# Attention stage of a decoder block: row maxima turned by a product in fp32r, and routing logits formed in four column groups

## What is computed

```
scores = einsum('bhqd,bhkd->bhqk', qh, kh) * scale
attn = softmax(scores, axis=-1)
out = einsum('bhqk,bhkd->bhqd', attn, vh)
x = x + concat @ Wo + bo
...
rh = gelu(layernorm(x) @ rW1 + rb1, approximate=False)   # 512 -> 1024
router_logits = rh @ rW2 + rb2                           # 1024 -> 4
```

## Time and profile before

| | us |
|---|---|
| median of 3 runs | 2783.26 (2781.48 to 2784.44) |
| profiled execution, its own time | 2773.2 |
| its span, first to last instruction | 2771.3 |
| mean granted TensorE clock | 0.935 of full |
| attention stage in the trace | about 1016 to 1851 |
| iterations 1 to 6, from the first scores of one to those of the next | 87.4, 90.0, 86.6, 87.0, 86.6, 86.6 |
| iteration 7; end after the last scores | 81.1; 65.2 |

### The profile page before, as it was taken

The page is one execution under the profiler, slowest core; times in us unless marked ns, Lnnn a source line. Parts: engine busy times, 40 slices in busy tenths (PEclk is TensorE's granted clock), DMA queues, the critical chain, the costliest instruction groups (busy, mean ns, idle before and its releaser), DMA issues. The chain is left out here.

```text
span 2771.3 us, 39110 instructions
## 1 busy us (share of the span) xinstructions
PE 2419.9 (87%) x14340; PEld 1986.3 (72%) x14340; DVE 1435.6 (52%) x1938; ACT 1220.4 (44%) x2631; POOL 1287.1 (46%) x868
## 2 busy tenths in 40 slices
PE   7999499999999974899999999851989989998991
PEld 6777388888888862566677667641878878888881
DVE  7714699999999961555566555531111121211213
ACT  4345377777777620344454444403333333333330
POOL 2323277777777730555555566508360450027004
PEclk9999699999999997799999999865999999999996
DMA  4327856666566545444555455138130130002025
GB/s 121 117 89 230 234 176 202 197 202 192 168 207 193 164 143 137 110 107 114 126 134 127 107 118 119 48 83 290 61 114 30 61 114 15 30 30 69 31 68 167
DMA packets 252357, 349.32 MB, mean 126 GB/s; under 512 B 36610, under 2 KB 176834, under 8 KB 251058
## 3 DMA queue, kind: packets, MB, share of 16 engines
q1 hardware_dynamic: 232866, 293.06, 37.7%
q0 software_dynamic: 12768, 43.52, 4.9%
q10 hardware_dynamic: 6576, 10.82, 1.1%
HBM read 215.97 MB, written 131.35 MB: 125 GB/s over the span
## 5 line engine op out<-in xcount | busy, mean ns | idle before, releaser
L764 POOL TENSOR_TENSOR s_hc<-s_h,s_Cc 128x896 f32<-128x896 f32 x256 | 495.4, 1940 | 202.7 <-DVE s_h L869 116.2
L869 DVE TENSOR_TENSOR_SCAN s_h<-s_decay,s_ub 128x928 f32<-128x928 f32 x256 | 527.5, 2080 | 11.1 <-ACT s_decay L799 2.8
L907 PE MATMUL s_yps<-s_hc,s_ident 128*128 128x224 f32 x2048 | 431.0, 354 | 1.0 <-POOL s_hc L764 1.0
L1865 DVE TENSOR_TENSOR e_hl<-e_ps,e_hh 128x256 fp32r<-128x256 f32 x256 | 108.8, 425 | 570.7 <-ACT e_ps L1911 570.7
L799 ACT ACTIVATE s_decay<-s_dt,s_A 128x224 f32<-128x224 f32 x1024 | 388.0, 470 | 18.3 <-DVE s_h L869 18.2
L1161 DVE TENSOR_REDUCE t_nmax<-t_ps 112x1 f32<-112x752 f32 x256 | 240.4, 939 | 283.5 <-PE t_ps L1381 282.7
L907 PEld LDWEIGHTS s_yps<-s_hc,s_ident 128*128 128x128 f32 x2048 | 369.3, 191 | 2.0 <-POOL s_hc L764 1.4
L1131 POOL TENSOR_TENSOR t_part<-t_pT 125x672 f32<-125x672 f32 x128 | 206.8, 1616 | 333.1 <-ACT t_pT L1308 331.0
L1937 PE MATMUL e_ps<-e_xTh,e_w1h 128*128 128x256 f32 x1024 | 292.1, 285 | 23.7 <-DVE e_xTl L1857 23.7
L1910 ACT ACTIVATE e_hh<-e_ps,e_b 128x256 fp32r<-128x256 f32 x256 | 121.9, 476 | 418.9 <-PE e_ps L1939 418.4
L1308 ACT ACTIVATE t_pT<-t_ps 125x448 f32<-125x448 f32 x384 | 181.3, 546 | 261.4 <-PE t_ps L1405 261.0
(11 more groups left out here) (206 smaller groups left out, 4334.8 us busy)
## 6 DMA issues: line engine op xcount, KB each, us to landing
s_ut<-ut_d SPq DMA_DIRECT2D x192, 128.0 KB, 3.3
e_stage<-in_L_ffn_We POOLq DMA_DIRECT2D x24, 1024.0 KB, 5.7
t_k<-kh_d SPq DMA_DIRECT2D x64, 375.0 KB, 6.3
xs_d<-s_zero SPq DMA_DIRECT2D x30, 512.0 KB, 3.3
ut_d<-a_x SPq DMA_DIRECT2D x32, 448.0 KB, 5.7
s_Cc<-cs_d SPq DMA_DIRECT2D x8, 1792.0 KB, 9.7
kh_d<-s_kh SPq DMA_DIRECT2D x32, 375.0 KB, 2.7
kl_d<-s_kl SPq DMA_DIRECT2D x32, 375.0 KB, 2.9
```

Source lines behind the costliest of these rows:

```text
L764: nc.gpsimd.tensor_tensor(hc[:, u % 2, k], h[:, u % 2, k, :, 2:SLOT], Cc[:, b % 2, k], ALU.mult).then_inc(hc_done, 1)
L869: nc.vector.tensor_tensor_scan(h[:, u % 2, k].rearrange("p n t -> p (n t)"), decay[:, u % 2, k].rearrange("p n t -> p (n t)"), ub[:, s % 2 ...
L907: ins = nc.tensor.matmul(yps[:, u % 2, 0:L], ident[:], hc[:, u % 2, :, n], start=(n == 0), stop=(n == NS - 1))
```

## The change

Two parts, on the tiles of the attention stage alone.

1. **Maxima.** `nmax` becomes fp32r, and a copy of the identity in fp32r, `turner`, is made once by ACT at the stage's start. The two products of `turn_max` use them. Nothing is moved.
2. **Logits.** `logit_parts` at step 4 has the operands exchanged: `rw2`, widened to 32 columns (4 of weights, 28 zeros), is stationary, and 224 tokens of `rh` are the moving operand. The eight products go to the four column groups in turn, two of them added in each group, so four partial sums stand in PSUM at partitions 0, 32, 64 and 96. ACT copies them to `lpart` (at the end of step 4). At step 5 two products add the four parts and bring the tokens to the partitions, with `lpart` stationary and a 128 x 4 matrix of zeros and ones, `pick`, moving. POOL makes `rw2`'s zeros and `pick` at the stage's start, and SP waits for the zeros ahead of the loads of `it` = -1, step 11. DVE's `hidden` waits for `lp_mm` instead of `lg_mm`.

```diff
-        nmax = sb("nmax", [TT, 2, HEADS])
+        nmax = sb("nmax", [TT, 2, HEADS], F32R)
+        turner = sb("turner", [TT, TT], F32R)
...
+                    sp.wait_ge(consts_set, 2)
...
+            nc.gpsimd.memset(rw2[:], 0.0).then_inc(consts_set, 1)
+            pool.wait_ge(first_loaded, 32)
+            nc.gpsimd.tensor_tensor(pick[:], ident[:, 0:E], ident[:, DK:DK + E], ALU.add).then_inc(consts_set, 1)
+            for n in (1, 2):
+                pool.wait_ge(consts_set, 2 + n)
+                nc.gpsimd.tensor_tensor(pick[:], pick[:], ident[:, (n + 1) * DK:(n + 1) * DK + E], ALU.add).then_inc(consts_set, 1)
...
                 if q == 0 and b >= 1:
-                    dve.wait_ge(lg_mm, 2 * b)
+                    dve.wait_ge(lp_mm, b)
...
+            def logit_parts(b):
+                act.wait_ge(lp_mm, b + 1)
+                if b >= 1:
+                    act.wait_ge(lg_mm, 2 * b)
+                nc.scalar.activation(lpart[:], ps[:, BANK5, 0:L], ACT.Copy).then_inc(lp_done, 1)
...
+            nc.scalar.activation(turner[:], ident[0:TT, 0:TT], ACT.Copy).then_inc(q_scaled, 1)
...
+                if sl == 4 and among(last, B):
+                    logit_parts(last)
...
                 for u in range(2):
-                    ins = nc.tensor.matmul(ps[0:2, TURN_BANK, u * TT:(u + 1) * TT], nmax[:, u, s % HEADS:s % HEADS + 2], ident[0:TT, 0:TT],
+                    ins = nc.tensor.matmul(ps[0:2, TURN_BANK, u * TT:(u + 1) * TT], nmax[:, u, s % HEADS:s % HEADS + 2], turner[:],
                                            start=True, stop=True)
...
-            def logits(b, u):
-                if u == 0:
-                    pe.wait_ge(rh_done, b + 1)
-                    pe.wait_ge(x1_done, 2 * batches(b + 4) - (b + 3 < B))
+            def logit_parts(b):
+                pe.wait_ge(rh_done, b + 1)
+                pe.wait_ge(x1_done, 2 * batches(b + 4) - (b + 3 < B))
                 for c in range(RC):
-                    ins = nc.tensor.matmul(ps[0:TT, BANK5, u * E:(u + 1) * E], rh[:, c, u * TT:(u + 1) * TT], rw2[:, c],
-                                           start=(c == 0), stop=(c == RC - 1))
-                ins.then_inc(lg_mm, 1)
+                    at = c % 4 * DK
+                    ins = nc.tensor.matmul(ps[at:at + DK, BANK5, 0:L], rw2[:, c], rh[:, c], start=(c < 4), stop=(c >= 4),
+                                           tile_position=(0, at))
+                ins.then_inc(lp_mm, 1)
+            def logits(b):
...
+                pe.wait_ge(lp_done, b + 1)
+                for u in range(2):
+                    nc.tensor.matmul(ps[0:TT, BANK5, L + u * E:L + (u + 1) * E], lpart[:, u * TT:(u + 1) * TT], pick[:],
+                                     start=True, stop=True).then_inc(lg_mm, 1)
...
-                if sl in (4, 5) and among(last, B):
-                    logits(last, sl - 4)
+                if sl == 4 and among(last, B):
+                    logit_parts(last)
+                if sl == 5 and among(last, B):
+                    logits(last)
```

More of the change, by code:

```diff
@@ L977, in attention @@
         wout, wq = sb("wout", [P, CC, DM]), sb("wq", [P, KC, DM])
-        wo, rw1, rw2 = sb("wo", [P, KC, DM]), sb("rw1", [P, KC, RH]), sb("rw2", [P, RC, E])
+        wo, rw1, rw2 = sb("wo", [P, KC, DM]), sb("rw1", [P, KC, RH]), sb("rw2", [P, RC, DK])
         bqc, bvc, rb1c = sb("bqc", [P, KC]), sb("bvc", [P, KC]), sb("rb1c", [P, RC])
@@ L998, in attention @@
         rh = sb("rh", [P, RC, L])
+        lpart, pick = sb("lpart", [P, L]), sb("pick", [P, E])
         lg = sb("lg", [TT, B, 2, E])
@@ L1007, in attention @@
         x2_stored, xn_stored, lg_stored = sem("x2_stored"), sem("xn_stored"), sem("lg_stored")
-        ones_set, rows_zeroed, rows_set, q_scaled = (sem(n) for n in ("ones_set", "rows_zeroed", "rows_set", "q_scaled"))
+        consts_set, rows_zeroed, rows_set, q_scaled = (sem(n) for n in ("consts_set", "rows_zeroed", "rows_set", "q_scaled"))
         score_mm, max_done, turn_mm, turn_done = (sem(n) for n in ("score_mm", "max_done", "turn_mm", "turn_done"))
@@ L1015, in attention @@
         q_mm, q_high, q_low = sem("q_mm"), sem("q_high"), sem("q_low")
-        rh_mm, rh_pre, rh_done, lg_mm, lg_done = (sem(n) for n in ("rh_mm", "rh_pre", "rh_done", "lg_mm", "lg_done"))
+        rh_mm, rh_pre, rh_done, lp_mm, lp_done, lg_mm, lg_done = (
+            sem(n) for n in ("rh_mm", "rh_pre", "rh_done", "lp_mm", "lp_done", "lg_mm", "lg_done"))
         N_W, N_REST = 4, 5
@@ L1112, in _ @@
                 if it == -1 and sl == 11:
-                    for dst, src in ((wo[:], rows(Wo)), (rb1c[:], rb1), (rw1[:], rows(rW1)), (rw2[:], rows(rW2)),
+                    sp.wait_ge(consts_set, 2)
+                    for dst, src in ((wo[:], rows(Wo)), (rb1c[:], rb1), (rw1[:], rows(rW1)), (rw2[:, :, 0:E], rows(rW2)),
                                      (rb2r[:], rb2.partition_broadcast(P))):
@@ L1123, in _ @@
         def _(pool):
-            nc.gpsimd.memset(ones[:], 1.0).then_inc(ones_set, 1)
+            nc.gpsimd.memset(ones[:], 1.0).then_inc(consts_set, 1)
+            nc.gpsimd.memset(rw2[:], 0.0).then_inc(consts_set, 1)
[4 more added lines that the diff above has]
+                nc.gpsimd.tensor_tensor(pick[:], pick[:], ident[:, (n + 1) * DK:(n + 1) * DK + E], ALU.add).then_inc(consts_set, 1)
             def row_sum(g):
@@ L1341, in _ @@
                 nc.scalar.activation(t[:], t[:], ACT.Copy, scale=float(DK) ** -0.5).then_inc(q_scaled, 1)
+            act.wait_ge(first_loaded, 32)
+            nc.scalar.activation(turner[:], ident[0:TT, 0:TT], ACT.Copy).then_inc(q_scaled, 1)
             act.wait_ge(q_scaled, 2)
@@ L1386, in turn_max @@
                 s = 2 * p
+                if p == 0:
+                    pe.wait_ge(q_scaled, 3)
                 pe.wait_ge(max_done, 2 * s + 4)
@@ L1423, in row_sums @@
                 if J == 0:
-                    pe.wait_ge(ones_set, 1)
+                    pe.wait_ge(consts_set, 1)
                 pe.wait_ge(sum_done, 4 * (J + 1))
```

4 lines of the change are left out of this document (3 added, 1 removed).

## The result

The kernel after takes 2752.35 us (median of 4 runs, 2745.87 to 2758.6) against 2783.85 us (4 runs, 2781.48 to 2786.54) for the kernel before on the same chip: ratio 0.9886, 95% interval 0.9861 to 0.9912. The forecast was 2756.1 us. In a second comparison it took 2750.36 us (6 runs) against 2782.23 (11 runs), ratio 0.9883, interval 0.9861 to 0.9904. The profiled execution of after took 2750.82 us, with a span of 2749.0.

The account below looks back on a forecast made before the run. PE was taken to bound iterations 1 to 6. Turns less keys 16.5, logits 3.1, iteration 7 2.0, end 1.7, iteration 0 0.5 and clock 3.4 sum to 27.2 us off 2783.26: 2756.1 us, range 2749 to 2769.

Parts of the forecast that it names:

- gap gone: Turn of the maxima on PE: with fp32r the gap around it goes, gaining 0.50 us a turn; 2756.1 us, chance 0.48.
- gap that stays: Rival: the gap around the 2-wide turn on PE remains with fp32r, gain 0.27 us a turn; 2761.3 us, chance 0.36.
- The turn: fp32r turns on PE gain 0.50 us among wide products, 0.28 where row sums follow, 0.24 in step 10; 2.86 per batch.
- Step 8 moves along with the turn: Step 8's chain over row sums, DVE and queries was to move with the turn, so its 0.28 us is kept.
- Logits, step 4: Step 4's eight logits products on PE, 1.50 us, were to take 1.02 with the full gap; gain 0.5 (0.45 to 0.7).
- Step 5: Eight logits products become two, but PE then waits for DVE's `residual1` ahead of the second projection; gain 0.1 us, not 1.1.
- The keys: Key transfers of steps 10 and 14 to 0, landing late for the scores, take back 0.1 us a batch.
- The clock: Iteration 2: no fall to clock 0.50 behind the logits once the thin products are replaced; gain 3.4 us.
- Iteration 7 and the end: Iteration 7 gains 2.0 us; after the last scores 1.7, of it 1.3 for the last logits, 0.4 for the batch before.
- Iteration 0: First iteration, where DVE and transfers bound: gain 0.5 us.
- The clock falls more often: Rival: PE idles more and gets the lower clock oftener, 3.4 us a fall; ten falls give 2793 us, slower; chance 0.05.

Follow-up runs that it names:

- experiment 2: Kernel after with the maxima in fp32 again, turned as the first 2 of 66 stationary columns, the other 64 zeros; 2768.61 us (one run).
- experiments 3 and 4: Kernel after with two unread products added behind the logits' products (2756.98 us); kernel after with DVE's o and oT of step 5 moved to step 4's end (2749.62 us).
- maxima alone: Kernel before with only the maxima and the small identity in the rounded format, logits as before; 2758.99 us (4 runs), ratio 0.9919.
- bias adds late: Kernel before with POOL's two bias adds of step 13 put behind that step's row sums; 2773.9 us (median of 9 runs), ratio 0.9964.
- combined kernel: Kernel after with EPS as bias of ACT's square root, step 5's o and oT early, POOL's bias adds late, step 0's keys by halves; 2733.57 us (5 runs).

## Why the prediction was right, and where it was not

The sign, the size (31.5 us against 27.2 by the medians; 22.3 by the two profiled spans) and the likeliest case were right. Two of its signs to tell the cases apart disagree: a step with a turn is 0.15 us longer than one without (2.21 against 2.06), as forecast for the gap gone, but the steady iterations of 83.7 to 84.1 us are nearer to the 84.0 forecast for the gap that stays than to 83.2, because the turns gave 0.56 us less than forecast in steps 0, 4, 8, 10 and 12 (0.28 of it in step 8). Step 4's parts take 0.89 us (about 1.0 forecast), and the wait in step 5 is 0.72 (about 1 forecast). By its own steps:

- **The turn.** 0.50 gained in steps 2, 6, 14: measured 0.51, 0.51, 0.52. 0.28 where row sums follow: 0.24, 0.20, 0.23, 0.23. 0.24 at most in step 10: 0.16. The gap is gone, and experiment 2 supports the stated reason. Here the Trainium skill, "PSUM — Partial Sum Buffer" (The four PSUM rules), said what the trace of before could not: its side remark that float32r products force the column group agrees with the 0.27 us.
- **Step 8 moves along with the turn**: wrong, and the step of the turns' sum that failed most. It gave 0.23 and lost 0.23 in step 9, six times: 1.4 us. The chain over row sums, DVE and queries holds an operation that ends with POOL's add, and POOL starts ahead of the turn. Step 0's 0.28 lost 0.06 to ACT's chain in step 1. So turns give 2.30 a batch, not 2.86.
- **Logits, step 4**: 0.5 forecast, 0.52 measured. **Step 5**: 0.1 forecast, 0 measured; that the 0.96 us become idle time ahead of the projection was the right reading of the earlier trace rows, and experiments 3 and 4 show it from both sides. It is what kept the forecast from 1.0 us a batch too much.
- **The keys**: 0.1 a batch forecast, 0.3 measured (1.6 us in the balance of six iterations). The late landings in the earlier trace rows were seen, but weighed by their median.
- **The clock.** No fall in iteration 2 after, as forecast, but worth 1.64 us and not 3.4. That the thin products make it fall is not shown: of the three traces that have them it fell there in two (before, maxima alone), and not in the kernel before with the bias adds late; in the nine without them it never fell there. The other 1.81 of that iteration's excess, and 1.75 in iteration 1, which I had not compared, were POOL's adds against oT. The term was put down to one cause because the low clock stood in the same iteration; the half-steps of iteration 2 against those of iteration 3 would have parted them: 4.41 against 2.77 in step 4 and 3.67 against 1.86 in step 13.
- **Iteration 7 and the end**: 2.0 and 1.7 forecast, 4.0 and 5.3 measured. In iteration 7 the largest single piece is 1.38 us in step 10's second half (4.58 to 3.20), of which the prediction had priced 0.24 at most. At the end the last logits gave 2.3 where 1.3 was forecast, and the batch before the last, given 0.4, gave 3.05: the mis-sized terms are its thin products and the projection behind them, shorter at a higher clock. Iteration 0: 0.5 forecast, none in this pair of traces; over all traces it runs from 102.6 to 107.0 us, and the kernel after alone has 106.0 and 103.8.
- **The rivals.** "The clock falls more often" was given 0.05, as a case that turns the sign. It exists as a small one: falls at step 9 in some executions of after, at 1.5 us each. Its price per fall was set at twice what it is.

The errors nearly cancel, and that is luck: the six iterations give 20.1 us where 23.0 were forecast with three terms too large (turns and keys 12.2 for 16.5, logits 2.6 for 3.1, clock 1.64 for 3.4) and one of 3.56 (step 13) not seen at all; the ends give 9.3 where 3.7 were forecast; and the 10 us between the runs of before and its profiled execution are no part of the reasoning.

The medians differ by 31.5 and the profiled spans by 22.3 because the profiled execution of before was 10 us below its median, while after's was within 2 of it. None of the 34 other runs of before was as short (2776.22 to 2793.76 against 2773.2). Where those 10 us lie no trace shows. Its first scores come earliest of all twelve traces, so part may lie there; it stays open. Open too is why the combined kernel's iteration 7 and end are 5.8 us shorter than those of the kernel after beside it: the mean clock in iteration 7 differs (0.86 against 0.83), but nothing was run that separates it.

## What to carry to other kernels

Compare two traces half-step by half-step at a mark that recurs, not by sums: an edit's gain shows to 0.02 us, and so does the place where it is given back. Before counting what comes back of time taken out on the busiest engine, find the chain over the other engines that ends just behind it, and ask for each of its operations whether it is anchored behind or ahead of the edit; the 0.96 us of step 5 and the 0.23 of step 8 were lost to such chains, and came back with one moved operation each. Keep small SBUF-to-SBUF steps of VectorE that sit on a chain away from GpSimd's long adds.
